# Attention scores from two-way fp32r halves in four 32-row quarters, with a reordered TensorE queue

## The reference, cut to what matters

```python
x = x + attn(layernorm(x))
x = x + ffn(layernorm(x))

# attn: q, k, v = split(xn @ w_qkv + b_qkv); 16 heads of 8
attn = einsum('bhqd,bhkd->bhqk', q, k) / sqrt(8)
attn = softmax(where(causal, attn, -inf))
out  = einsum('bhqk,bhkd->bhqd', attn, v) @ w_proj + b_proj

# ffn: 8 experts, hidden 512
probs = sigmoid(xn @ Wg + bg);  weights = probs * (probs > 0.5)
h = relu(xn @ W1[e] + b1[e]);   y = h @ W2[e] + b2[e]
out = sum over e of weights[:, e] * y[e]
```

## Time and profile before

| | |
|---|---|
| median of 3 runs | 763.07 us (762.34 to 765.86) |
| profiled execution | 762.58 us, span 760.8 us |
| first z matmul of the first expert layer | 108.12 us |
| VectorE, ScalarE, GpSimd busy | 69%, 54%, 36% |

### The profile page before, as it was taken

How to read it: one execution, slowest core, us unless ns; L and a number is a source line. 1 busy time by engine, 2 the same in 40 slices (tenths; PEclk the granted TensorE clock), 3 DMA queues, 4 the chain that set the end, 5 groups by cost and what they waited for, 6 DMA issues and landing times.

```text
span 760.8 us, 13160 instructions
## 1 busy us (share of the span) xinstructions
PE 723.6 (95%) x4515; PEld 413.8 (54%) x4515; DVE 528.3 (69%) x1044; ACT 407.4 (54%) x745; POOL 276.2 (36%) x424
## 2 busy tenths in 40 slices
PE   2969999999999999999999999999999999999996
PEld 2323345566555655555555645556455655567764
DVE  7977787678666786668865687666766676537543
ACT  1355665546555565556555655556545565654442
POOL 4173243334333343235422443333323433333232
PEclk9959999999999999999999999999999999999998
DMA  5521113110231122110221112111221101200300
GB/s 173 146 59 48 48 39 92 53 52 15 56 84 44 37 67 66 51 37 16 67 78 52 26 35 86 45 44 25 66 65 52 38 2 36 65 28 2 96 28 15
DMA packets 37698, 40.63 MB, mean 53 GB/s; under 512 B 5920, under 2 KB 26280, under 8 KB 37632
## 3 DMA queue, kind: packets, MB, share of 16 engines
q1 hardware_dynamic: 37104, 39.60, 18.9%
q10 hardware_dynamic: 528, 0.20, 0.2%
HBM read 23.52 MB, written 2.23 MB: 34 GB/s over the span
## 4 chain that ended last, share of the span: by engine, by line
PE 87%; DVE 4%; SPq 3%; issue 2%; ACT 2%; POOL 1%; DMA 0%; POOLq 0%; DVEq 0%; ACTq 0%
PE pv_bank L1160 11%; PE y_bank L1211 10%; PE z_bank L1026 10%; PE z_bank L1028 8%; PE y_bank L1215 8%; PE z_bank L1027 8%; PE y_bank L1213 8%; PE ring L1085 6%; PE ring L1082 6%; PE ring L1032 5%; PE ring L1098 5%; SPq L567 3%; PE ring L1139 1%; PE ring L1175 1%; PE ring L1026 1%
## 5 line engine op out<-in xcount | busy, mean ns | idle before, releaser
L794 ACT ACTIVATE h_hi<-z_bank 128x512 fp32r<-128x512 f32 x256 | 153.3, 599 | 186.3 <-PE z_bank L1028 159.9
L991 DVE SCALAR_TENSOR_TENSOR h_lo<-z_bank,h_hi 128x512 fp32r<-128x512 f32 x224 | 153.5, 686 | 86.7 <-ACT h_hi L794 85.4
L763 ACT ACTIVATE pt<-ring 128x512 f32<-128x512 f32 x292 | 163.9, 598 | 54.0 <-PE ring L1085 53.8
L941 DVE TENSOR_REDUCE negmax<-ring 128x1 f32<-128x512 f32 (+1 forms) x173 | 115.7, 683 | 43.3 <-PE ring L1098 43.1
L682 POOL TENSOR_SCALAR_AFFINE_SELECT pt<-pt 128x512 f32<-128x512 f32 x128 | 81.0, 645 | 153.5 <-ACT pt L763 153.2
L1211 PE MATMUL y_bank<-h_hi,w_lo 128*128 128x512 f32 x256 | 118.5, 463 | 2.4 <-POOL h_lo L689 1.8
L1026 PE MATMUL z_bank<-x2T_lo,w_hi 128*128 128x512 f32 x256 | 112.6, 440 | 0.2
L699 POOL TENSOR_TENSOR f_buf<-f_buf 128x512 f32<-128x512 f32 x56 | 71.9, 1284 | 107.9 <-DVE f_buf L1002 107.8
L1215 PE MATMUL y_bank<-h_lo,w_hi 128*128 128x512 f32 x256 | 101.1, 395 | 0.0
L1028 PE MATMUL z_bank<-x2T_hi,w_hi 128*128 128x512 f32 x256 | 101.0, 395 | 0.0
L1213 PE MATMUL y_bank<-h_hi,w_hi 128*128 128x512 f32 x256 | 100.6, 393 | 0.0
(11 more groups left out here) (171 smaller groups left out, 835.2 us busy)
## 6 DMA issues: line engine op xcount, KB each, us to landing
f_buf<-gates SPq DMA_DIRECT2D x64, 256.0 KB, 3.3
stack<-parts SPq DMA_DIRECT2D x192, 64.0 KB, 2.1
x_in<-in_L_attn_x SPq DMA_DIRECT2D x8, 256.0 KB, 3.1
pt<-in_L_ffn_W SPq DMA_DIRECT2D x1, 2048.0 KB, 10.0
out_x<-f_buf SPq DMA_DIRECT2D x8, 256.0 KB, 2.4
stack<-stack SPq DMA_DIRECT2D x32, 32.0 KB, 1.9
stack<-nmT SPq DMA_DIRECT2D x64, 6.0 KB
wqkv_in<-in_L_attn_w_qkv ACTq DMA_DIRECT2D x1, 192.0 KB, 3.2
```

The source lines that it names most:

```text
L763: sc.activation(pt[:, slot, :], b[:], ACT.Exp, scale=SCALE).then_inc(free_sem("ex", i, g, u), 1)
L794: sc.activation(h_hi[:, (i * SLOTS + s) % 3, :], z_bank[s % 2][:], ACT.Relu).then_inc(s_hhi, 1)
L941: v.tensor_reduce(dst, src, AX.X, ALU.max, negate=True).then_inc(free_sem("max", i, g, u), 1)
L991: v.scalar_tensor_tensor(out=h_lo[:, (i * SLOTS + s) % 3, :], in0=z_bank[s % 2][:], scalar=0.0, in1=h_hi[:, (i * SLOTS + s) % 3, :].bitcas ...
```

## The change

Scores are made from two-way fp32r halves. `parts` has a high and a low half of q and of k; three products (high by high, high by low, low by high) are interleaved in 32 rows a head together with one row for the negative maximum, so that four heads fit into four quarters of the array: group parity picks the half (rows 0 to 63 or 64 to 127), head parity the quarter in it. The q/k chain loses its GpSimd step and its second VectorE step. A stack is four DMAs, the maxima are one. `nm` is two GpSimd instructions, and the transpose is four fp32r matmuls with `nm` (128 columns) as weights and `ident32` as the moving operand. In a block all first products are issued before the second ones. `POOL_SPLITS` has 8 slots a sequence, and `h_all` has one buffer.

```diff
-Q_PART = (0, 0, 1, 0, 1, 2)
-K_PART = (0, 1, 0, 2, 1, 0)
-M_SLOT = 6
+Q_PART = (0, 0, 1)
+K_PART = (0, 1, 0)
+M_ROW = 3
+M_STEP = 16
-STACK_DMAS = 7
+STACK_DMAS = 4
-POOL_SPLITS = [s for s in range(SLOTS) if s % 8 == 7]
+POOL_SPLITS = [s for s in range(SLOTS) if s % 4 == 3]
-SWITCH = 100
+UNIT_COST = 230
+ENTER = {"full": 190, "mask": 92, "scores": 190, "pv": 98}
 SWITCH_DUE = 0.3
+PV_DUE = 0.3
+HALF_DUE = 2
...
-            put("dve", (qk + "rest", i), t0 - 14.8 + n, 750, ("act", (qk, i)))
-            put("pool", (qk + "part", i), t0 - 14.7 + n, 700, ("dve", (qk + "rest", i)))
-            put("dve", (qk + "part", i), t0 - 14.6 + n, 690, ("pool", (qk + "part", i)))
+            put("dve", (qk + "lo", i), t0 - 14.8 + n, 750, ("act", (qk, i)))
...
+        cost += UNIT_COST * (2 if mx and ex and (mx[0][2] - ex[0][2]) % 2 == 0 else 1)
...
         if pairs and free >= 2:
-            due = min(p[0] for p in pairs.values()) + (SWITCH_DUE if mode != "rows64" else 0)
+            due = min(p[0] for p in pairs.values()) + (SWITCH_DUE if form == "full" else 0)
+            if free < 4 or len(pairs) == 1:
+                due += HALF_DUE
             if best is None or due < best[0]:
+                if pv and form == "full":
+                    start(now, "pe", pv[1])
+                    return
...
-        stack = sb("stack", [P, PAIRS, 2, T], BF16)
+        stack = sb("stack", [P, GROUPS // 2, 2, 2, T], F32R)
...
+                    rows = stack[64 * (g % 2):64 * (g % 2) + 64, g // 2].bitcast(F32)
                     for s, (a, b) in enumerate(zip(Q_PART, K_PART)):
-                        sp.dma_start(stack[s::8, heads, :, :],
-                                     parts[32 * g:32 * g + 32, a:4 + b:3 + b - a, :]
+                        sp.dma_start(rows[s::4, :, :, :],
+                                     parts[32 * g:32 * g + 32, a:3 + b:2 + b - a, :].bitcast(F32)
                                      ).then_inc(s_stack[g], 16)
...
+                    hi, lo = [nm[:, :, 0:8].rearrange("p t (r k n) -> p t r k n", r=2, k=2)[:, :, :, k, :]
+                              for k in range(2)]
+                    g_.tensor_copy(hi, negmax[:, g]).then_inc(s_nmstep, 1)
+                    pool.wait_ge(s_nmstep, n + 1)
+                    g_.tensor_tensor(lo, negmax[:, g], hi.bitcast(F32),
+                                     ALU.subtract).then_inc(s_nm, 1)
...
-            v.memset(stack[:, :, 0, :], 0.0).then_inc(s_stackset, 1)
-            v.memset(stack[:, :, 1, :], 1.0).then_inc(s_stackset, 1)
+            blocks = stack[:].bitcast(F32).rearrange("p a b n t -> p (a b) n t")
+            v.memset(blocks[:, :, 0, :], 0.0).then_inc(s_stackset, 1)
+            v.memset(blocks[:, :, 1, :], 1.0).then_inc(s_stackset, 1)
+            v.memset(nm[:].bitcast(F32), 0.0).then_inc(s_stackset, 1)
...
+            def head_rows(g, j):
+                r = 64 * (g % 2) + 32 * (j % 2)
+                return stack[r:r + 32, g // 2, j // 2]
...
+                for k in range(2):
+                    for last_form, unit, pieces in units:
+                        if k >= len(pieces):
+                            continue
+                        out_, lhsT, rhs = pieces[k]
+                        stop = last_form and k == len(pieces) - 1
+                        last = mm(out_, lhsT, rhs, start=(k == 0), stop=stop, skip_group_check=True)
...
-                    four_transposes(b[:].bitcast(BF16)[0:12, 0:T],
-                                    lambda t: nm16[:, g, t].rearrange("p r k n -> p (r k n)"),
-                                    ident16[:]).then_inc(done, 1)
+                    for t in range(TB):
+                        last = mm(b[:, t * P:(t + 1) * P], nm[:, t, :], ident32[:], start=True, stop=True)
+                    last.then_inc(done, 1)
```

More of the change, by code:

```diff
@@ L239, in list_schedule @@
     emptier = {}
-    mode = "rows128"
+    form = "full"
     def at(time, what, key):
@@ L254, in start @@
     def start(now, engine, key):
-        nonlocal mode, banks
+        nonlocal form, banks
         cost = work[key][1]
@@ L260, in start @@
         if engine == "pe":
-            if mode != "rows128":
-                cost += SWITCH
-            mode = "rows128"
+            new = "pv" if item[0] == "pv" else "full"
+            if form != new:
+                cost += ENTER[new]
+            form = new
             if item[0] not in ("z", "y", "pv"):
@@ L308, in pick_pe @@
                 continue
-            if item[0] not in ("z", "y", "pv") and not free:
+            if item[0] == "pv":
+                if pv is None or due < pv[0]:
+                    pv = (due, key)
+                continue
+            if item[0] not in ("z", "y") and not free:
                 continue
```

180 lines of the change are left out of this document (78 added, 102 removed).

## The result

The change makes the kernel slower: median 776.28 us (four runs, 776.10 to 781.36) against 763.12 us before (four runs, 762.34 to 765.86), a ratio of 1.0182 with a 95% interval of 1.0134 to 1.023. The profiled execution has a span of 774.5 us where that of before had 760.8, so 13.7 us are to be found. The forecast was 758 us: wrong in its direction, although the measured time lies inside its outer range of 740 to 785 us.

A forecast was written before the change was run, and what follows sets the result against it. TensorE's queued work bounds the kernel from 108 us, the start's handover before that. Span 760.8 - 4.6 (start) + 1.8 (work) - 1.0 (last layer) = 757.0, profiled 758.8, forecast 758 us; range 740 to 785, its own 750 to 766.

The forecast's parts named there:

- TensorE's work behind the first z: TensorE's queue after the first z slot: 1.8 us more of the +7.7 us total work.
- queued loads: Rival at every block: row quarters load weights one after the other, +60 us, near 815; chance 0.09.
- short products: Rival at score blocks and `nm`: 128-column fp32r products take four passes, near 788 us; chance 0.06.
- the second load: Rival in two-product units: the second product's load waits for the first, 18 us more, near 776; chance 0.03.
- hidden loads: Rival at entries into scores: bare loads hide, the 22.5 us are not paid, 731 to 745 us; chance 0.15.
- Tail: Last expert layer: VectorE's sum over a slot falls with low halves on GpSimd, 1 us less.
- SP and the first ex: Start: fewer SP issues and shorter VectorE work bring ex units to 44 instead of 51.5 us, 7.5 us earlier.
- From first ex to first z: Start on TensorE: 52.1 us of work plus 7.5 us loss, first z at 103.6, 4.6 us earlier.
- the 7.5 us kept for waits and half clock: Between first ex and first z: loss of some 10.7 us before, with 3.4 us taken out.
- the start doesn't shorten: Rival in the start: VectorE full, half clock stays, first z about 108, 763 to 768 us; chance 0.17.

The follow-up runs named there:

- e4: Changed kernel with 4 low halves a sequence on GpSimd instead of 8, order planned anew; 780.81 us.
- e1: Changed kernel with VectorE's normalisation of sequence 2 moved behind the maxima of group 2, unit 3; 772.57 us.
- e6: Changed kernel with extra stretches of bare pairs, masked pairs, masked fours and pv between full products at TensorE's end; only masked 32-row pairs fell to 0.50 clock.
- e11: Kernel before with five end stretches of 40 product pairs, varying rows, type, masks and a full product; no whole time given, first z at 107.6 us.
- e14: Changed kernel, order and waits kept, with score products contracting 64 rows instead of 32 ahead of the first z; 767.5 us.
- e18: Control of e14: changed kernel with the same constant tiles but 32 rows ahead of the first z; 777.9 us.
- e19: The kernel of e14 once more, timed in rounds; median 766.58 us, 1.0049 of the kernel before.
- e15: Changed kernel with both the 64 rows of e14 and the moved normalisation of e1; 764.0 us.
- e16: Kernel before with the stack's ones cleared as fp32 words and W2's load behind four stacks on SP, other queues unchanged; 771.04 us, 1.0103 of before.
- e17: Kernel before with only the stack's ones cleared as fp32 words of two bf16 ones; 761.0 us, 0.9967 of before.

## Why the prediction was wrong, point by point

**TensorE's work behind the first z: right.** The pitches came as worked out: 0.11 for the bare load at every block, 0.44 for eight products in four quarters, no queue of loads, no dearer short product, no wait before the second product. The sum said +1.8 us from z to z, measured is nothing (591.37 and 591.34); `nm` at 0.39 instead of 0.43 is a part of it. The rivals on queued loads (815), short products (788), the second load (776) and hidden loads (731 to 745) all fall by the rows of the block, although the one on the second load named 776, the measured time: that nearness is chance.

**Tail.** Taken at -1 us. From the first product of the last z slot of sequence 6 to the last y it is 54.1 us before and 55.3 after, +1.2. The cause was not tested; eight GpSimd slots with a single `h_all` are a candidate (e4 with four slots and a new plan has 53.9).

**SP and the first ex: half right.** The maxima went out at 42.77, near the 42 named. The first ex product was to come at 44 and came at 47.86. This failed at a wait that the sum didn't have: I followed the maxima through five engines, but not the ring banks that the ex products need. These hung on reductions behind a normalisation that had met GpSimd's W2 work: 4.64 us for what took 1.11. 3.1 us came back when it was moved (e1: first ex product at 44.75).

**From first ex to first z: the failed step.** "Now the work there is 52.1 us." and "I take 3.4 us (half of 51.5 to 58.2) out of the loss and keep 7.5." Forecast 59.6 us, measured 73.2 (47.86 to 121.10). TensorE alone in that stretch of the changed kernel (busy us and count, granted clock, DMA share, GB/s):

```profile
47.86:121.10 73.24, 68.97 (x464) 0.72 0.15 34
```

It is idle for 4.3 us, and some 39 of the busy 69 us are at half clock. Taking half of these off leaves an estimate of 49.7 us of work at the full clock, 2 less than the 52.1 of the sum. So the term that failed is the 7.5 us kept for waits and half clock, which measured some 23.5 by the same estimate: 4.3 idle and 19.3 of half clock. The work was right, its clock was not.

I had taken half clock as the echo of a wait of 2.8 us, to shrink as the stacks land earlier. They did: the second stack's first issue came at 23.61 instead of 28.92, its last at 29.93 instead of 38.25, TensorE's wait for a stack was 1.04 us (at 34.22) instead of 2.78, and the half clock grew. Nor was it the wait of 4.14 us ahead of the first ex product: in e1 that is 1.03 us, and 44.4 us are at half clock. e6 shows the changed kernel's max half block falling to 0.50 with no wait at all, e11 that it takes 32 rows together with fp32r and its bare load, and e14 with e18 and e19 that in the whole kernel the 32 rows cost 10 us. So the bare load was priced at 0.11 us each in the sum, rightly, and the 32-row fp32r block had a second price that no row of before could show: in the earlier trace rows a block stands between z and y slots of three full products each, where the clock holds. The start has no z or y slots between its blocks.

Two slips in the sum change nothing: 10.7 less 3.4 is 7.3, not 7.5, and 108.12 less 103.6 is 4.5, not 4.6.

**The rival that ended slower** in the start, "the start doesn't shorten", gave 763 to 768 us by half clock that stays. It didn't think of half clock that grows. The errors sum up: 17.5 us at the first z, -1.8 from z to z, +2.2 to the last y and -0.5 behind it (6.7 us after, 7.2 before), 17.4 against 17.5 measured (774.5 - 757.0).

**Open.** Why the chip grants less to 32-row fp32r pairs than to 64-row ones at the same pitch isn't shown, only that it does, nor what in the gaps between the products of a block counts. No run prices the 5 us that e15 leaves to the forecast.

## What to carry to other kernels

Packing a product into fewer rows keeps its pitch, but it can cost the granted clock where such blocks follow each other closely; in e11 one full product in each block was not enough to hold it, among z and y slots it held. Run the new pattern by itself, forty times between stretches of full products, before trusting a sum of pitches, and price each stretch by what stands around it there. When a step gets earlier, follow the buffers that the next one needs as well as its data, and when a load is moved, move what waits for it on the other engines.

## What the runs showed of the hardware that was not expected

- TensorE's granted clock fell to 0.50 in stretches without a wait: pairs of 32-row fp32r products with two masks (0.64 us a pair; e6 and e11), and with one full product and no mask (0.86 us; e11). It stayed at 1.00 for 32-row bf16 pairs (0.54), 64-row fp32r pairs (0.65), four quarters with masks (0.77), pairs with masks and a full product (0.93), and bare pairs in a row (0.23).
- Four VectorE `TENSOR_SCALAR` of 128x128 fp32 took 4.64 us beside fp32 subtractions on GpSimd and 1.11 us elsewhere, while GpSimd's own pace was 6.17/5 = 1.23 us, as elsewhere (2.52/2 in e16). That VectorE pays and GpSimd doesn't is the row's. The Trainium skill ("SBUF — State Buffer", section "SBUF: two separate sides") says that GpSimd's instructions and some of VectorE's share a pair of ports, which one instruction holds to its end while the other is blocked. The trace agrees: each of the four takes about one GpSimd instruction (4.64/4 = 1.16) and ends 0.08 us behind the end of one.
- A clear of 4096 bf16 took 3.47 us, the same bytes as 2048 fp32 words 1.76 us, with two bf16 ones in a word. The Trainium skill ("VectorE: DVE Perf Modes", "Zero memsets can be issued as uint32") has this for zeros, since a clear pays by the element. The trace agrees, half the elements take half the time (1.76 of 3.47), and e17 shows it for a value that isn't zero.
- The changed kernel's start varied by 5 us at its first z from one execution to another (121.1, and 115.7 in e6), the steady part behind it by 0.3 us (591.3 and 591.6).
